# Decoder on one core: bank table, split inverses and a later output projection in the second attention

## The reference

```python
qkv = x @ W_qkv + b_qkv                      # 16 heads of 16 columns
scores = einsum('bhqd,bhkd->bhqk', q, k) * 16**-0.5
attn = softmax(scores, axis=-1)
out = einsum('bhqk,bhkd->bhqd', attn, v)     # back to (2, 1024, 256)
x = layernorm(x + out @ W_proj + b_proj)
```

## Time and profile before

| what | value |
|---|---|
| three runs | 2716.95, 2717.26, 2713.73 us (median 2716.95) |
| the profiled execution | 2717.37 us; its span 2715.5 us |
| PE busy over the span | 2450.4 us, 90%, 13518 matmul records |
| DVE busy | 1686.8 us, 62% |
| ACT, POOL busy | 1250.1 us (46%), 886.2 us (33%) |
| line 1507, the naturals' maxima | 512 times, 333.1 us, mean 683 ns |
| line 1420, the exponentials | 256 times, 248.2 us, mean 1022 ns |
| second self-attention, natural halves | from 1893.2 to 2388.4 us |

### The profile page before, as it was taken

How to read it: one execution, slowest core, us unless ns; L and a number is a source line. 1 busy time by engine, 2 the same in 40 slices (tenths; PEclk the granted TensorE clock), 3 DMA queues, 4 the chain that set the end, 5 groups by cost and what they waited for, 6 DMA issues and landing times.

```text
span 2715.5 us, 35197 instructions
## 1 busy us (share of the span) xinstructions
PE 2450.4 (90%) x13518; PEld 1709.8 (63%) x13520; DVE 1686.8 (62%) x3009; ACT 1250.1 (46%) x1967; POOL 886.2 (33%) x462
## 2 busy tenths in 40 slices
PE   8999998999999879899999999998899999966662
PEld 7555545744554569788888888897455555534521
DVE  5566664376666355877443443345878788856967
ACT  4555554354555234344444444443466565632442
POOL 3776775265777350102220221101400000004423
PEclk9999999999999989899999999998899999987875
DMA  2000001000000030001000010001343333301000
GB/s 76 12 13 24 12 12 43 13 12 14 22 12 8 16 117 1 32 1 32 32 16 17 32 40 1 9 1 41 87 90 80 88 75 71 73 10 29 1 1 31
DMA packets 57431, 88.08 MB, mean 32 GB/s; under 512 B 13992, under 2 KB 37808, under 8 KB 57264
## 3 DMA queue, kind: packets, MB, share of 16 engines
q1 hardware_dynamic: 57120, 85.77, 12.3%
q10 hardware_dynamic: 144, 0.07, 0.0%
HBM read 37.16 MB, written 2.10 MB: 14 GB/s over the span
## 4 chain that ended last, share of the span: by engine, by line
PE 71%; DVE 20%; issue 3%; ACT 3%; POOL 2%; DMA 1%; SPq 0%; ACTq 0%; DVEq 0%; POOLq 0%
PE PS L85 70%; DVE s_nm L1507 4%; DVE m_gl L1096 2%; DVE PS L575 2%; DVE a_QS L553 1%; ACT a_P L518 1%; DVE a_nm L567 1%; DVE X L270 1%; DVE s_T L1479 1%; DVE x_E L1916 1%; DVE x_rd L1900 1%; DVE st_s L231 1%; POOL f_H L2121 1%; POOL a_sum L675 1%; ACT a_QS L472 0%
## 5 line engine op out<-in xcount | busy, mean ns | idle before, releaser
L675 POOL TENSOR_TENSOR a_sum<-a_sum,a_P 128x1024 f32<-128x1024 f32 x192 | 456.4, 2377 | 128.3 <-ACT a_P L518 118.0
L1096 DVE TENSOR_TENSOR m_gl<-m_g,m_gh 128x512 fp32r<-128x512 f32 x288 | 258.0, 901 | 386.7 <-ACT m_g L935 386.7
L518 ACT ACTIVATE a_P<-PS 128x512 f32<-128x512 f32 x512 | 290.2, 596 | 354.0 <-PE PS L85 349.2
L932 ACT ACTIVATE m_gh<-PS,cols 128x512 fp32r<-128x512 f32 x288 | 198.5, 689 | 469.5 <-PE PS L85 469.5
L1507 DVE TENSOR_REDUCE s_nm<-PS 128x1 f32<-128x512 f32 x512 | 333.1, 683 | 89.6 <-PE PS L85 86.9
L567 DVE TENSOR_REDUCE a_nm<-PS 128x1 f32<-128x1024 f32 x256 | 300.2, 1215 | 127.5 <-PE PS L85 127.5
L85 PE MATMUL PS<-m_w2h,m_gh 128*128 128x256 f32 x1152 | 324.5, 282 | 18.8 <-DVE m_gl L1096 18.7
L85 PE MATMUL PS<-m_w2l,m_gh 128*128 128x256 f32 x1152 | 323.0, 280 | 0.0
L85 PE MATMUL PS<-m_w2h,m_gl 128*128 128x256 f32 x1152 | 322.9, 280 | 0.0
L1420 ACT ACTIVATE s_P<-PS 128x1024 f32<-128x1024 f32 x256 | 248.2, 1022 | 106.4 <-PE PS L85 105.9
L85 PE MATMUL PS<-a_P,a_V 128*64 128x512 f32 x1024 | 250.5, 611 | 0.0
(11 more groups left out here) (296 smaller groups left out, 4198.0 us busy)
## 6 DMA issues: line engine op xcount, KB each, us to landing
m_raw<-in_m_w SPq DMA_DIRECT2D x16, 1024.0 KB, 5.0
s_Q<-s_T SPq DMA_DIRECT2D x128, 128.0 KB, 2.4
s_K<-s_T SPq DMA_DIRECT2D x128, 128.0 KB, 2.4
a_KH<-a_KH SPq DMA_DIRECT2D x64, 128.0 KB, 2.4
a_wr<-in_w_qk SPq DMA_DIRECT2D x16, 256.0 KB, 2.8
X<-in_x SPq DMA_DIRECT2D x4, 512.0 KB, 6.2
a_P<-in_w_v SPq DMA_DIRECT2D x8, 256.0 KB, 5.8
a_P<-in_w_o SPq DMA_DIRECT2D x2, 1024.0 KB, 5.9
```

Source lines behind the costliest of these rows:

```text
L518: e.activation(a_P[:, g % N_P, half * 512:half * 512 + 512], PS[:, 2 + half, :], ACT.Exp).then_inc(s["a_exp"], 1)
L675: e.tensor_tensor(o[:, :], a_P[:, (g - 1) % N_P, :] if k == 1 else o[:, :], a_P[:, g % N_P, :], ALU.add).then_inc(s["a_add"], 1)
L932: e.activation(m_gh[r][:, :], PS[:, 4 + n % 3, :], func, bias=cols[:, bcol:bcol + 1]).then_inc(s["m_gh"], 1)
L1096: e.tensor_tensor(m_gl[r][:, :], m_g0[r][:, :], m_gh[r][:, :].bitcast(F32), ALU.subtract).then_inc(s["m_gl"], 1)
```

## The change

Three things change, all in this stage.

1. Banks 0, 1 and 7 are shared. A table is worked out while the program is built: in PE's order, each natural half or piece gets, of the three banks, the one whose last user is read earliest in DVE's order; it waits for that user's reader. Of the 128 rounds with naturals, 67 still give n2 the bank of the same round's n0, as before; these are the rounds where a piece has taken a bank. In the others the natural waits for the one three before it.
2. Inverses are of 64 columns in place of 128: 16 for each of the first three groups, one in each round from 11 to 26 (mod 32) from round 43 on; before there were 8, in rounds 11 to 16, 18 and 20. GpSimd's multiplication comes with round 27 (mod 32), before 22.
3. The output projection of batch 0 stands in rounds 95, 98, 102, 105 (before 89, 91, 93, 95), its two norms behind 98 and 105 (before 91 and 95), the turned pieces in 107, 109, 114, 117 (before 105, 107, 109, 111).

The number of matmuls stays; DVE gets 24 reciprocals more (48 of 64 columns for 24 of 128).

```diff
-            if u in (89, 91, 93, 95):
-                side[u].append(("project", u - 89))
-                if u % 4 == 3:
-                    side[u].append(("norm", u - 91))
-            if u in (105, 107, 109, 111):
-                side[u].append(("turned", (u - 105) // 2))
-            if 43 <= u < 128 and u % 32 in (11, 12, 13, 14, 15, 16, 18, 20):
-                side[u].append(("inverse", (u - 42) // 32, 128 * (11, 12, 13, 14, 15, 16, 18, 20).index(u % 32), 128))
+            if u in (95, 98, 102, 105):
+                i = (95, 98, 102, 105).index(u)
+                side[u].append(("project", 2 * i))
+                if i % 2:
+                    side[u].append(("norm", 2 * i - 2))
+            if u in (107, 109, 114, 117):
+                side[u].append(("turned", (107, 109, 114, 117).index(u)))
+            if 43 <= u < 128 and 11 <= u % 32 < 27:
+                side[u].append(("inverse", (u - 43) // 32, 64 * (u % 32 - 11), 64))
...
+        bank, bank_free, last_use = {}, {}, {0: (-1, ("s_i", 12)), 1: (-1, ("s_i", 12)), 7: (-1, (who_old, n_old))}
+        for u in range(N_R + 1):
+            uses = [("natural", 4 * u + i) for i in range(4)] if 2 * u < N_K else []
+            for what in uses + (side[u] if u < N_R else rest):
+                if what[0] not in ("inverse", "divide", "norm"):
+                    bk = min(last_use, key=lambda k: last_use[k][0])
+                    bank[what], bank_free[what] = bk, last_use[bk][1]
+                    last_use[bk] = (place[what], ended[what])
...
-                if z >= 2:
-                    e.wait_ge(s["s_nr"], z - 1)
-                else:
-                    e.wait_ge(s["s_i"], 12)
-                mm(e, PS[:, half, :], Qs[n % R_S][:, i * 128:(i + 1) * 128],
+                who, v = bank_free["natural", z]
+                e.wait_ge(s[who], v)
+                mm(e, PS[:, bank["natural", z], :], Qs[n % R_S][:, i * 128:(i + 1) * 128],
...
-                e.wait_ge(s[i7_free[what][0]], i7_free[what][1])
+                bk, (who, n) = bank[what], bank_free[what]
+                e.wait_ge(s[who], n)
...
-                if u >= 54 and u % 32 == 22:
-                    g = (u - 54) // 32
+                if u >= 59 and u % 32 == 27:
+                    g = (u - 59) // 32
...
-                        e.wait_ge(s["s_b7"], n_b7["inverse", g, half * 512 + 384, 128])
+                        e.wait_ge(s["s_b7"], n_b7["inverse", g, half * 512 + 448, 64])
```

More of the change, by code:

```diff
@@ L25 @@
               "c_kT c_sub c_s c_E c_e0 c_aT c_vd c_et c_ol c_o m_w2 m_g0 m_a m_gl m_fin m_y m_gate c_l2 m_p7 c_exp c_oh "
-              "m_gh m_h7 m_gT c_l0 rows c_xb m_b7 m_r1 m_w1 m_r2 s_wrl s_w s_z1 s_wpl s_g0 s_g1 s_g2 s_g3 s_nr s_i s_n "
-              "s_exp s_st s_b7 s_za s_pv s_red s_zm s_p7 s_ip s_hi s_zd0 s_zd1 s_mhd f_l0 f_l1 f_iv f_qv s_xb f_qp x_lk "
+              "m_gh m_h7 m_gT c_l0 rows c_xb m_b7 m_r1 m_w1 m_r2 s_wrl s_w s_z1 s_wpl s_g0 s_g1 s_g2 s_g3 s_n s_exp s_i "
+              "s_st s_b7 s_za s_pv s_red s_zm s_p7 s_ip s_hi s_zd0 s_zd1 s_mhd f_l0 f_l1 f_iv f_qv s_nr s_xb f_qp x_lk "
               "x_kv x_lv x_vd x_pl x_ql x_q x_fp x_ft x_ev x_z x_lo x_zT x_o x_n0 x_n1 x_t x_K0 x_K1 x_min x_s x_qh x_sub "
@@ L1244, in program @@
         rest = [rest[i] for i in (0, 1, 3, 4, 2, 6, 7, 5)] + [("norm", 8)] + [rest[i] for i in (9, 10, 8, 11)] + [("norm", 12)]
[L1245 to L1255, removed]
-                count[who] += 1
[L1257 to L1260, removed]
+        order = []
+        for u in range(N_R + 1):
+            n = [("natural", 4 * u + i) for i in range(4)] if 2 * u < N_K else []
+            now = [w for w in side[u] if w[0] == "values"] if u < N_R else []
+            order += n[0:3] + ([w for w in side[u - 1] if w[0] != "values"] if u else []) + n[3:4] + now
+        order += rest
+        place, i7, n_b7, ended = {}, {}, {}, {}
+        count = {"s_b7": 0, "s_nr": 0, "t_xl": 16}
+        for what in order:
+            if what[0] != "norm":
+                who = {"natural": "s_nr", "turned": "t_xl"}.get(what[0], "s_b7")
+                count[who] += 1
+                place[what], n_b7[what], ended[what] = len(place), count[who], (who, count[who])
+        bank, bank_free, last_use = {}, {}, {0: (-1, ("s_i", 12)), 1: (-1, ("s_i", 12)), 7: (-1, (who_old, n_old))}
+        for u in range(N_R + 1):
+            uses = [("natural", 4 * u + i) for i in range(4)] if 2 * u < N_K else []
[4 more added lines that the diff above has]
+                    last_use[bk] = (place[what], ended[what])
+                    if what[0] not in ("natural", "turned"):
+                        i7[what] = len(i7) + 1
         def pe_l1a(e):
@@ L1329, in piece @@
                     return
-                bk = bank7[what]
-                e.wait_ge(s[i7_free[what][0]], i7_free[what][1])
+                bk, (who, n) = bank[what], bank_free[what]
+                e.wait_ge(s[who], n)
                 if what[0] == "rows":
                     e.wait_ge(s["s_red"], what[1] + 1)
-                    t = e.transpose(PS[0:8, 7, 0:128], s_nm[:, what[1] % 2, :], ident[:, :])
+                    t = e.transpose(PS[0:8, bk, 0:128], s_nm[:, what[1] % 2, :], ident[:, :])
                 elif what[0] == "values":
                     for i in range(2):
-                        t = values(1, what[1] + i, 7, 256 * i)
+                        t = values(1, what[1] + i, bk, 256 * i)
                 elif what[0] == "proj":
@@ L1341, in piece @@
                         e.wait_ge(s["s_w"], 2 * (g + 2))
-                    t = proj(g, u, 7)
+                    t = proj(g, u, bk)
                 elif what[0] == "turned":
                     e.wait_ge(s["normed"], 48 + 2 * what[1] + 2)
-                    turned(what[1], 7)
+                    turned(what[1], bk)
                     return
@@ L1433, in act_l1a @@
                             e.wait_ge(s[f"row{h % 2}"], 256 + 32 * (h // 2))
-                        e.activation(s_mh[:, h % 2, :], PS[0:8, 7, 0:128], ACT.Copy).then_inc(s["s_mhd"], 1)
+                        e.activation(s_mh[:, h % 2, :], PS[0:8, bank[what], 0:128], ACT.Copy).then_inc(s["s_mhd"], 1)
                     elif what[0] == "proj":
                         e.wait_ge(s["s_p7"], i7[what])
-                        proj(what[1], what[2], 7)
+                        proj(what[1], what[2], bank[what])
                     elif what[0] == "turned":
-                        turned(what[1], 7)
+                        turned(what[1], bank[what])
             for i in range(4, 8):
@@ L1506, in natural @@
                     e.wait_ge(s["s_red"], n - 1)
-                e.tensor_reduce(nm2[:, n % 2, i, half:half + 1], PS[:, half, :], AX.X, ALU.max,
+                e.tensor_reduce(nm2[:, n % 2, i, half:half + 1], PS[:, bank["natural", z], :], AX.X, ALU.max,
                                 negate=True).then_inc(s["s_nr"], 1)
@@ L1519, in piece @@
                 elif what[0] == "turned":
-                    turned(what[1], 7)
+                    turned(what[1], bank[what])
                 elif what[0] == "proj":
-                    low(what[1], what[2], 7).then_inc(s["s_b7"], 1)
+                    low(what[1], what[2], bank[what]).then_inc(s["s_b7"], 1)
                 elif what[0] == "inverse":
@@ L1537, in piece @@
                         e.wait_ge(s["s_mhd"], h + 1)
-                        t = e.tensor_tensor(s_ml[:, h % 2, :], PS[0:8, 7, 0:128], s_mh[:, h % 2, :].bitcast(F32), ALU.subtract)
+                        t = e.tensor_tensor(s_ml[:, h % 2, :], PS[0:8, bank[what], 0:128], s_mh[:, h % 2, :].bitcast(F32), ALU.subtract)
                     elif what[0] == "values":
-                        t = values(what[1], 2, 7)
+                        t = values(what[1], 2, bank[what])
                     else:
-                        jj, bk = what[1], bank7[what]
+                        jj, bk = what[1], bank[what]
                         e.wait_ge(s["s_xb"], jj + 2)
```

## The result

| | before | after |
|---|---|---|
| median of the runs | 2715.34 us (2710.94 to 2717.26, 4 runs) | 2683.61 us (2681.74 to 2687.32, 4 runs) |
| profiled execution; its span | 2717.37; 2715.5 us | 2684.54; 2682.3 us |
| second self-attention, naturals | 495.2 us | 467.0 us |

The ratio is 0.9887 with a 95% interval of 0.987 to 0.9904: 1.1% faster. The forecast was 2696.5 us in a range of 2687 to 2710.

A forecast was written before the change was run, and what follows sets the result against it. The prediction took PE's waits for two banks as the bound of quiet rounds. Nine stretch terms summed to 20.5 us off the profiled 2717.37, giving 2696.9, or 2696.5 as median; range 2687 to 2710.

The forecast's parts named there:

- q: Quiet round: n2 waits for the reader of n0, and the pipe restarts; priced at 0.26 us.
- m: Round behind the last step of a head's maxima (every fourth), which delays n0's reader; priced at 0.46 us.
- p: Round behind one with a `proj` reader; priced at 0.45 us, 0.42 with the spread between rounds.
- idle PE behind `s_b7` in a round without an inverse: Profile sign that would show the prediction wrong: PE idle on `s_b7` where no inverse stands; no size given.
- a tie: Rounds with a 64-column inverse: DVE's work, 3.0 to 3.2 us with extras, about equals PE's 3.05 to 3.1.
- b: Piece waiting for the piece before it in bank 7: start 0.5 us late, 0.9 when `proj` follows `values`.
- DVE's crowding: Rounds 89 to 105: layernorm steps put off the maxima around round 98; its removal was part of 5.5 us gained.
- restarts: Rounds 89 to 105: one round of restarts added to the 67.9 us sum, giving 68.7.
- DVE bounds the full rounds: Rounds 0 to 16: eight rounds with weight pieces need 3.3 to 3.4 us of DVE, above PE's 3.05.
- Half of it: Rival: DVE's lateness uses up the third bank in stretches with inverses and norms; 8.5 us remain, 2708; chance 0.19.
- The waits only change place: Rival: naturals wait where pieces did, only q and m gain; within 5 us of no change, 2714; chance 0.08.
- Slower: Rival: naturals wait on late piece readers, 31 us lost against 20.5 gained, 2728; chance 0.06.

The follow-up runs named there:

- e7: Kernel after with the pieces' readers moved from behind n2 to right behind n0, in the table and on DVE; 2676.8 us.
- e4: Kernel after with inverses of 128 columns in their old rounds and GpSimd's old place, the projection left late; 2690.4 us.
- e1: Kernel after with inverses, GpSimd's place and the projection put back, so the bank table alone; 2687.5 us.
- e3: Kernel before with only the later projection, norms and turned pieces, old banks and inverses; 2717.2 us.
- e12: Kernel after with every piece kept in bank 7 and the naturals free to take 0, 1 or 7; 2699.9 us.
- e10: Kernel after with each maximum over 256 of the 512 columns, leaving out half of the keys; 2661.0 us, one run.
- e11: Kernel after with naturals kept in banks 0 and 1 and pieces free to take 0, 1 or 7; 2752.9 us.

## Why the forecast missed

**Right.** The two banks bound the quiet rounds: they take 3.02 to 3.06 us, forecast 3.05, and the stretch without inverses or norms gained 2.7 against 2.8. The prices of q and m held (rounds 26 and 28: 3.30 to 3.02, 3.54 to 3.08), and p was a little higher than 0.42 (rounds 19 and 23: 4.88 to 4.38, 4.86 to 4.40). Round 36 kept its length, 3.61 and 3.58, with the wait moved to n0; e7 shows that cause by removing it. (The prediction also named idle PE behind `s_b7` in a round without an inverse as a sign of being wrong. Round 36 has it, 0.27 us, and it is the wait at n0 that the same paragraph expects; the two signs contradict each other.) The inverse of 64 columns takes 540 ns, forecast 0.54. So its fixed part is real, but 24 more instructions bring no net loss: from round 9 on the stage takes 432.5 us with the table and both other edits, 436.5 without the small inverses (e4) and 433.8 without either (e1). In this case the advice of the Trainium skill ("VectorE: DVE Perf Modes", the TRN2 errata) against small tiles reading SBUF does not decide, since DVE's time lay beside PE's; what the small inverses cost, 0.8 and 0.7 us in rounds 49 to 64 and 81 to 88, came from their place ahead of a reader.

**Wrong: the sum, by 7.7 us in the stage.** The mechanism was right; the step that failed is the sizing of the terms in the sum, above all of those in which the prediction takes DVE's lateness off what the banks give. Seven of the nine were too low; rounds 17 to 32 and 113 to 127 came out as forecast, within 0.1 us:
- Rounds 33 to 48, forecast 2.9, measured 3.6. I called the rounds with an inverse a tie and let the halved inverses free 0.1 us. They freed 0.7 (after against e1 and e4): rounds 46 to 48 took 3.04 to 3.09 us.
- Rounds 49 to 64 and 81 to 88, forecast 1.0 and -1.0, measured 1.9 and 0.0. Where an inverse precedes the reader, the loss was 0.34 a round, not 0.46, and rounds 51 and 55 gained 0.2 beside it.
- Rounds 65 to 80, 6.3 against 7.5: the pieces' waits for one another (b) in rounds 69 to 72, with the q in 71, were worth 4.7 us by the round lengths (25.6 to 20.9). I had 4.0, and then 0.3 off for round 73, which lost 0.15.
- Rounds 89 to 105, 5.5 against 6.8. DVE's crowding was less than half of it: the later projection alone gives 2.7 (e3), the table alone 2.4 (e1), and 3.7 of the whole hangs on the pieces sharing banks (e12). I had added the rounds up to 67.9 us, which was within 0.5 of the measured 67.4, and then put 0.8 on top for restarts that no row asked for.
- Rounds 106 to 112, -2.3 against -1.0. DVE is nearly the limit there (25.1 of 27.0 us busy, e10 3.8 us shorter). My list of its work was too long, 28.3 us. Counted from start to start, DVE's instructions fill 25.1 us of the stretch: the norm's steps 4.2 where I had 5.6, the maxima 16.7 where I had 17.8 (27 of the 28 fall into it), the inverses 2.0 for 2.3, `rows` and last steps 0.4 for 0.8, the three readers 1.8 as forecast.
- Rounds 0 to 16, 2.7 against 4.2. Rounds 9 to 16 gave 1.65 us where 1.7 was put. Rounds 0 to 8 gave 2.6 where 1.0 was put, some 0.6 of it the clock. That DVE bounds the full rounds was wrong in part: the full rounds 10 and 11 took 3.04 and 3.06 us after.
- Rounds 113 to 127 met 2.6 by luck. By 3.1 us a round the stretch would have taken about 46 us, not the 48.4 that 2.6 gained means, so the term did not follow from its working. And rounds 113 to 119 took 3.4 us on average; the table alone gained 3.7 there (e1), and the later norm and turned pieces took 1.2 back.

One reading was wrong as well, without weight in the sum: DVE is busy for 75 to 91% of the stretches, not 78 to 91 (51.69 of 68.97 us in rounds 65 to 80).

The rest of the miss lies outside the edited stage: the profiled execution of before, 2717.37 us, stood at the top of its runs, and its parts outside the stage took 5.0 us more than those of after. With the 7.7 us alone the forecast would have been missed at 2688.8 us, still inside the range. That the time fell below the range was thus partly chance, the spread of code that nobody changed.

**The range.** Its lower end, 2687, allowed 8 us for rounds 89 to 112 and the first nine. It left out that all terms could be low together, and that the base itself, one profile, is uncertain by some 5 us.

**The rivals.** "Half of it" assumed that DVE's lateness eats what the bank gives wherever inverses and norms stand; each of its stretches gained (3.6, 1.9, 6.8 and 2.6 us). DVE's lateness is still there, though: halving the maxima takes 21.8 us off the stage (e10), 11 of them outside rounds 0 to 16 and 106 to 112. "The waits only change place" holds for the `rows` rounds behind a `proj` (20, 24, 36, 40 and the like) and no more. "Slower" named the right mechanism, naturals that lack a bank because a piece holds it; e11 shows what decides: it came when the naturals kept two banks and pieces could take them (36 us slower than before by the profiles' stages), not with three.

What stays open: the split of rounds 0 to 8 between table and clock is an estimate, and why the granted clock differs there from one execution to the next no run shows.

## What to carry to other kernels

Where a producer stands between two buffers and its reader has time to spare, a third buffer is worth the restart as well as the wait: here 0.26 us of 3.31 in each quiet round. If the third is taken from other users, share all of it by order of reading; sharing only one way can leave the main stream with less than it had. Then look at what now waits on the lent buffer, and put its reader into the gap where the reading engine idles: that was worth a further 7.3 us from round 9 on.

## What the runs showed of the hardware

The same instructions outside the edited stage took between 2211.4 and 2221.4 us over the profiles, with the granted clock of the spans between 0.952 and 0.956. The same first nine rounds took 37.0 us at a granted clock of 0.77 and 39.1 at 0.65.

A matmul that had waited cost some 0.1 us more than its wait. Round 28 before, n1, n2 and weigh:

```profile
2001.19 0.39 PE L85 MATMUL PS<-s_K,s_Q 128*128 128x512 f32 x1
2001.78 0.49 PE L85 MATMUL PS<-s_K,s_Q 128*128 128x512 f32 x1 [0.20 <-DVE s_nm L1507]
2002.20 0.42 PE L85 MATMUL PS<-s_P,s_V 128*32 128x256 f32 x4
```

Weigh followed the waiting n2 by 0.42 us, and by 0.43 in e11's lines above; in a free round n1 to weigh is 0.55 with 0.23 of it from n1 to n2, so 0.32 us. In this way some 0.16 us of waiting made a quiet round 0.26 us longer.

Three sizes of the reciprocal, 64, 128 and 256 columns, took 540, 941 and up to 1752 ns: 6.3 ns for a column and 0.14 us for each instruction. 48 of the first for 24 of the second caused no net loss beside a PE that was busy for 90 to 100% of each stretch.
